# Weight splits and rotary tables made once in the global stage and fetched at layer borders, with the last global norm placed beside the first units

## What is computed

```python
h = _layernorm(x) * (1 + ca) + sa
x = x + ga * attention(h, Wq, bq, Wk, bk, Wv, bv)   # one head, all 1024 tokens
h = _layernorm(x) * (1 + cb) + sb
x = x + gb * ffn(h)
# ffn: six layers, each
y = attn_layer(shift_tokens(y), Wqkv[i], ...) + y   # 16 heads of 64, windows of 32 with the one before
y = ffn_layer(shift_tokens(y), W1[i], W2[i], ...) + y
```

## Time and profile before

| | us |
|---|---|
| median of 3 executions (3318.55 to 3324.52) | 3323.32 |
| the profiled execution | 3324.42 |
| its span, first to last instruction | 3322.6 |
| TensorE busy (matmuls) | 3216.3, 97% |
| VectorE busy | 2647.6, 80% |
| ScalarE busy | 2454.8, 74% |
| GpSimd busy | 2301.0, 69% |
| HBM read / written | 20.48 MB / 2.10 MB |

### The profile page before, as it was taken

The page is one execution under the profiler, slowest core; times in us unless marked ns, Lnnn a source line. Parts: engine busy times, 40 slices in busy tenths (PEclk is TensorE's granted clock), DMA queues, the critical chain, the costliest instruction groups (busy, mean ns, idle before and its releaser), DMA issues. The chain is left out here.

```text
span 3322.6 us, 149878 instructions
## 1 busy us (share of the span) xinstructions
PE 3216.3 (97%) x62645; PEld 2548.6 (77%) x62645; DVE 2647.6 (80%) x6351; ACT 2454.8 (74%) x5069; POOL 2301.0 (69%) x1518
## 2 busy tenths in 40 slices
PE   7979999999999999999999999999999999999997
PEld 5758878777877777887877787777788777778775
DVE  4658878878888887887877888878888887888884
ACT  3437877777777777777777777778777777777774
POOL 2028777777777776777777777777777777777771
PEclk9989999999999999999999999999999999999998
DMA  2001111211211211211121111121111121111111
GB/s 88 3 3 52 46 41 48 70 40 41 56 46 41 74 42 41 55 45 43 49 66 42 48 49 46 41 71 45 48 47 45 43 68 46 50 41 49 46 41 49
DMA packets 98287, 158.06 MB, mean 48 GB/s; under 512 B 18128, under 2 KB 39632, under 8 KB 96720
## 3 DMA queue, kind: packets, MB, share of 16 engines
q1 hardware_dynamic: 93440, 132.73, 14.7%
q10 hardware_dynamic: 4176, 15.74, 1.4%
HBM read 20.48 MB, written 2.10 MB: 7 GB/s over the span
## 5 line engine op out<-in xcount | busy, mean ns | idle before, releaser
L315 POOL TENSOR_TENSOR qks<-work 128x1024 f32<-128x1024 f32 x384 | 911.2, 2373 | 106.4 <-issue 99.3
L323 POOL TENSOR_TENSOR qkr<-qks,rnorm 128x1024 f32<-128x1024 f32 x384 | 732.0, 1906 | 319.3 <-issue 236.1
L492 ACT ACTIVATE sq<-psum 128x512 f32<-128x512 f32 x768 | 460.3, 599 | 307.9 <-PE psum L734 286.8
L331 POOL TENSOR_TENSOR probn<-prob,psumr 128x512 f32<-128x512 f32 x384 | 401.0, 1044 | 310.0 <-DVE psumr L1104 309.9
L734 PE MATMUL psum<-whi,xhi 128*128 128x512 f32 x1152 | 552.2, 479 | 25.9 <-POOL xlo L340 19.2
L1056 DVE TENSOR_REDUCE ssq<-sq 128x8 f32<-128x512 f32 x768 | 518.8, 676 | 8.1 <-ACT sq L492 7.9
L1080 DVE TENSOR_TENSOR work<-psum,rot 128x512 f32<-128x512 f32 x768 | 508.0, 661 | 9.3 <-POOL qks L315 7.2
L757 PEld LDWEIGHTS psum<-kT,qTs 64*32 64x32 f32 x24576 | 362.9, 107 | 155.5 <-issue 128.0
L1098 DVE TENSOR_REDUCE psumr<-prob 128x8 f32<-128x512 f32 x384 | 261.7, 682 | 268.3 <-ACT prob L544 265.2
L734 PE MATMUL psum<-whi,xlo 128*128 128x512 f32 x1152 | 459.4, 399 | 0.0
L734 PE MATMUL psum<-wlo,xhi 128*128 128x512 f32 x1152 | 456.3, 396 | 0.0
(11 more groups left out here) (129 smaller groups left out, 6111.7 us busy)
## 6 DMA issues: line engine op xcount, KB each, us to landing
vsh<-vtok SPq DMA_DIRECT2D x384, 192.0 KB, 2.4
vsh<-vtok SPq DMA_DIRECT2D x384, 64.0 KB, 2.4
xsh<-xs_in SPq DMA_DIRECT2D x192, 64.0 KB, 2.4
ff_x<-x_mid SPq DMA_DIRECT2D x96, 128.0 KB, 2.4
wqkv<-Wqkv_dram ACTq DMA_DIRECT2D x5, 1536.0 KB, 7.4
wo_next<-Wo_dram ACTq DMA_DIRECT2D x5, 512.0 KB, 10.1
xtok<-x_dram SPq DMA_DIRECT2D x4, 512.0 KB, 11.1
out_dram<-qkr SPq DMA_DIRECT2D x8, 256.0 KB, 2.6
```

The costliest lines, as they stand in the source:

```text
L315: pool.tensor_tensor(qks[:, :, :], rcos, rsin, ALU.add).then_inc(s["add_ready"], 1)
L323: pool.tensor_tensor(qkr[:, n % 2, :, :], qks[:, :, :], rnorm[:, :].unsqueeze(2).to_broadcast([P, 2 * OCT, DH]), ALU.mult).then_inc(s["qkr ...
L331: pool.tensor_tensor(probn[:, :, :], prob[:, n % 2, :, :], psumr[:, n % 2, 1, :].unsqueeze(2).to_broadcast([P, OCT, KEYS]), ALU.mult).then ...
L492: act.activation(sq[:, w * OCT:(w + 1) * OCT, :], bank[w].rearrange("p (h n) -> p h n", n=DH), ACT.Square).then_inc(s[("sqq_ready", "sqk_r ...
```

## The change

All splits and all rotary tables are made by GpSimd in the global stage. Wqkv is laid out on the host in the order of SECTIONS, and fetched in 18 pieces (three a layer) of two sections, through two slots of wraw. GpSimd copies a piece to the high part and subtracts it for the low part (weights_split). The first layer's go to wparts, the later ones' to wstage, from where SP stores them to DRAM (wsplit, 15 stores of 1 MB). Tables of six layers (rotary_gains) go the same way, through rstage to rsplit, the first straight to rot, which is now a whole layer's. Around each border SP fetches six sections, two halves of the table and wo straight into place. wraw, wstage and their like share memory with buffers of the units (kT, vtok, qTs, aoT, qks, prob, probT), so GpSimd waits for the last stores before it clears those (overlays_set).

The statistics and the norm of the next batch come one tile earlier in VectorE's program. The last norm of the last batch goes to its own buffer, xn_last, and its parts stand in the units' loop: VectorE at the end of step 1, TensorE and ScalarE at the end of step 2. xlo of unit 0 comes before its rstd on GpSimd. Value projection of unit 0 waits for it.

```diff
-        rot_raw = sb("rot_raw", [P, TPB, 2, 2, DH])
-        rot = sb("rot", [P, TPI, 2, 2, DH])
-        wqkv = sb("wqkv", [P, 3, INNER])
-        whi = sb("whi", [P, 3, INNER], F32R)
-        wlo = sb("wlo", [P, 3, INNER], F32R)
-        wo_next = sb("wo_next", [P, INNER // P, D])
+        rot = sb("rot", [P, TPB, 2, 2, DH])
+        wparts = sb("wparts", [P, len(SECTIONS), 2, 512], F32R)
+        xn_last = sb("xn_last", [P, TPB, D])
...
@@ SP @@
-            sp.dma_start(wqkv[:, :, :].rearrange("p k n -> p (k n)"), Wqkv[0]).then_inc(s["wqkv_in"], 16)
+            def raw_fetched(j):
+                layer, k = j // PIECES, j % PIECES
+                sp.dma_start(wraw[:, j % 2, :, :].rearrange("p s n -> p (s n)"), Wqkv[layer][:, k * 1024:(k + 1) * 1024]).then_inc(wraw_in[j % 2], 16)
+            def split_stored(j):
+                layer, k = j // PIECES, j % PIECES
+                sp.dma_start(wsplit[layer - 1, 2 * k:2 * k + 2].rearrange("s p n -> p s n"),
+                             wstage[:, j % 2, :, :, :].bitcast(F32).rearrange("p s h n -> p s (h n)")).then_inc(w_stored[j % 2], 16)
+            raw_fetched(0)
+            raw_fetched(1)
...
+            for layer in range(1, DEPTH):
+                sp.wait_ge(s["rot_made"], layer + 1)
+                sp.dma_start(rsplit[layer - 1], rstage[:, layer % 2, :, :].rearrange("p t n -> p (t n)")).then_inc(r_stored[layer % 2], 16)
+            for j in range(DEPTH * PIECES):
+                sp.wait_ge(s["w_lo"], j + 1)
+                if j + 2 < DEPTH * PIECES:
+                    raw_fetched(j + 2)
+                if j >= PIECES:
+                    split_stored(j)
+            def section_renewed(layer, k):
...
+                sp.wait_ge(s[("projq_ready", "projk_ready", "vp_ready")[w]], layer * UNITS - 1 + oc)
+                sp.dma_start(wparts[:, k, :, :].bitcast(F32).rearrange("p h n -> p (h n)"), wsplit[layer - 1, k]).then_inc(wparts_in[k], 16)
+            def rotation_renewed(layer, half):
...
+                sp.wait_ge(s["rotk_ready"], layer * UNITS - (1 - half) * UNROLL)
...
+            def output_renewed(layer):
...
+                sp.wait_ge(s["wo_ready"], layer * TILES)
...
             for step in range(STEPS + 2 * UNROLL):
                 x_half(step)
+                section_renewed(renewed_at(step, 0), SECTION_AT[1, 1])
                 ffn_fetched(block_at(step, 1))
                 values_shifted(step - 4)
+                rotation_renewed(renewed_at(step, -6), 0)
+                section_renewed(renewed_at(step, -2), SECTION_AT[0, 0])
+                section_renewed(renewed_at(step, -2), SECTION_AT[1, 0])
+                section_renewed(renewed_at(step, -1), SECTION_AT[0, 1])
+                section_renewed(renewed_at(step, 1), SECTION_AT[2, 0])
+                section_renewed(renewed_at(step, 2), SECTION_AT[2, 1])
+                rotation_renewed(renewed_at(step, 2), 1)
+                output_renewed(renewed_at(step, 6))
@@ GpSimd @@
+            def rotary_gains(layer):
+                if layer >= 3:
+                    pool.wait_ge(r_stored[layer % 2], 16 * ((layer - 1) // 2))
...
+            def weights_split(j):
+                layer, k, slot = j // PIECES, j % PIECES, j % 2
+                pool.wait_ge(wraw_in[slot], 16 * (j // 2 + 1))
+                if j in (PIECES, PIECES + 1):
+                    pool.wait_ge(r_stored[1], 16 * 3)
+                    pool.wait_ge(r_stored[0], 16 * 2)
+                elif layer:
+                    pool.wait_ge(w_stored[slot], 16 * ((j - PIECES) // 2))
+                parts = wstage[:, slot, :, :, :] if layer else wparts[:, 2 * k:2 * k + 2, :, :]
+                pool.tensor_copy(parts[:, :, 0, :], wraw[:, slot, :, :]).then_inc(s["w_hi"], 1)
+                pool.wait_ge(s["w_hi"], j + 1)
+                pool.tensor_tensor(parts[:, :, 1, :], wraw[:, slot, :, :], parts[:, :, 0, :].bitcast(F32), ALU.subtract).then_inc(s["w_lo"], 1)
             global_inverse(0)
-            for k in range(len(SECTIONS)):
-                weights_low(0, k)
-            for n in range(1, 2 * B):
-                global_inverse(n)
+            pool.wait_ge(s["gain_in"], 16 * 2)
+            pool.wait_ge(s["gvs_ready"], 2)
+            for layer in range(4):
+                rotary_gains(layer)
+            global_inverse(1)
+            pool.wait_ge(s["gxn_ready"], 2)
+            for layer in range(4, DEPTH):
+                rotary_gains(layer)
+            done = 0
+            for n, pieces in ((1, 2), (2, 3), (3, 3), (4, 3), (5, 3), (6, 4)):
+                if n > 1:
+                    global_inverse(n)
+                    pool.wait_ge(s["gxn_ready"], n + 1)
+                for j in range(done, done + pieces):
+                    weights_split(j)
+                done += pieces
+            for half in range(2):
+                pool.wait_ge(w_stored[half], 16 * ((DEPTH * PIECES - PIECES + half) // 2))
+            pool.memset(kT[:, :, 0:WIN], 0.0)
+            pool.memset(vtok[:, 1, :, :], 0.0).then_inc(s["overlays_set"], 1)
+            x_low(0)
+            global_inverse(2 * B - 1)
...
             for step in range(STEPS + 2 * UNROLL):
-                low_renewed(renewed_at(step, -1), 0, 1)
-                low_renewed(renewed_at(step, 0), 2, 3)
-                low_renewed(renewed_at(step, 2), 4)
-                low_renewed(renewed_at(step, 3), 5)
-                rotary_gains(step)
-                x_low(step)
+                if step:
+                    x_low(step)
@@ ScalarE @@
-                weights_fetched(renewed_at(step, -8))
-                output_renewed(renewed_at(step, 6))
-                high_renewed(renewed_at(step, -1), 0, 1)
-                high_renewed(renewed_at(step, 0), 2, 3)
-                high_renewed(renewed_at(step, 2), 4)
-                high_renewed(renewed_at(step, 3), 5)
...
+                if step == 2:
+                    for half in range(2):
+                        normed_second(B - 1, half)
@@ TensorE @@
-                if n % UNITS < UPT:
-                    pe.wait_ge(s["w_lo"], n // UNITS * len(SECTIONS) + ((0, 1), (2, 3), (4, 5))[oc if w < 2 else 2][w if w < 2 else oc] + 1)
+                if n % UNITS < UPT and n >= UNITS:
+                    pe.wait_ge(wparts_in[SECTION_AT[w, oc]], n // UNITS * 16)
...
+                if n == 0 and w == 0:
+                    pe.wait_ge(s["overlays_set"], 1)
...
@@ VectorE @@
-                    if i in (3, 4) and b + 1 < B:
+                    if i in (2, 3) and b + 1 < B:
...
-                    if i == 5 and b + 1 < B:
+                    if i == 4 and b + 1 < B:
                         global_normed(b + 1)
...
             global_stats(B - 1, 0, TPB)
-            global_normed(B - 1)
...
                 rotation(step, 0)
+                if step == 1:
+                    global_normed(B - 1)
```

More of the change, by code:

```diff
@@ L52 @@
 SECTIONS = ((0, 0), (1, 0), (0, 1), (1, 1), (2, 0), (2, 1))
+SECTION_AT = {wo: k for k, wo in enumerate(SECTIONS)}
+PIECES = len(SECTIONS) // 2
 HALF = 2 * P
@@ L185, in build @@
         vsh_in = [sem(f"vsh_in{k}") for k in range(2 * UPT)]
+        wraw_in = [sem(f"wraw_in{k}") for k in range(2)]
+        w_stored = [sem(f"w_stored{k}") for k in range(2)]
+        r_stored = [sem(f"r_stored{k}") for k in range(2)]
+        wparts_in = [sem(f"wparts_in{k}") for k in range(len(SECTIONS))]
+        rot_in = [sem(f"rot_in{k}") for k in range(2)]
         block = ctx.enter_context(nc.Block())
@@ new lines, in _, with x_low @@
+            for half in range(2):
+                pool.wait_ge(w_stored[half], 16 * ((DEPTH * PIECES - PIECES + half) // 2))
+            pool.memset(kT[:, :, 0:WIN], 0.0)
+            pool.memset(vtok[:, 1, :, :], 0.0).then_inc(s["overlays_set"], 1)
+            def x_low(n):
+                if not is_unit(n) or n % 4:
+                    return
+                h = n // 4 % 2
+                part = (slice(None), slice(2 * h, 2 * h + 2), slice(None))
+                pool.wait_ge(s["xhi_ready"], n // 4 + 1)
+                pool.tensor_tensor(xlo[part], xsh[:, h, :].rearrange("p (a n) -> p a n", n=P), xhi[part].bitcast(F32),
+                                   ALU.subtract).then_inc(s["xs_ready"], 1)
@@ L449, in _ @@
                         normed_second(b - 1, i - 2)
-                    if i in (1, 2, 3) and b == 0:
-                        weights_high(0, 2 * i - 2)
-                        weights_high(0, 2 * i - 1)
                     if i == 7 and b + 1 < B:
@@ L455, in _ @@
                             projected(b + 1, n)
-            for half in range(2):
-                normed_second(B - 1, half)
             def attended(n):
@@ L796, in value_projection @@
                 need(pe, "vs_ready", n)
+                if n == 0:
+                    pe.wait_ge(s["gout_ready"], 2 * B)
                 if n % 2:
@@ L902, in _ @@
                 ffn_up(block_at(step, 3))
+                if step == 2:
+                    for half in range(2):
```

(1 more changed line is left out.)

135 lines of the change are left out of this document (57 added, 78 removed).

## The result

| | before | after |
|---|---|---|
| median, us | 3321.44 (4 executions, 3318.55 to 3324.52) | 3278.81 (4 executions, 3277.31 to 3282.98) |
| ratio, 95% interval | | 0.9874 (0.9856 to 0.9891) |
| profiled execution, its span | 3324.42, 3322.6 | 3280.10, 3278.3 |

The forecast was 3282, made from a profiled execution of 3324.42 and a median of 3323.32 over three executions; with a fourth the median of before is 3321.44. The changed kernel is 1.26% faster, and between the profiled spans 44.3 us are gone where the sum said 41.6. The three terms of that sum came out unequally, so the traces are read term by term.

What follows compares the result with a forecast made beforehand. TensorE, busy 97% of the span, was taken as the bound, with gains only where it waits. Borders -36, global stage -2.7 and seam -2.9 sum to -41.6 from 3324.4: 3282.8, for the median 3282, range 3262 to 3306.

Steps and rivals of the forecast that it cites:

- The bound: Whole kernel: TensorE sets a rhythm of 62.51 us per round; work taken from other engines counts only where TensorE waits.
- Borders, -36: Five layer borders: 40 us winnable by removing splits, wo copy and wqkv fetch, less 0.8 each; -25 to -43.
- rival 4: Layer borders: the 43 us are TensorE's own work in another order, so nothing goes there; 3319 us, chance 0.04.
- The 0.6 for the W1/W2 fetch: Layer borders: estimated 0.6 us per border left to ffn_renewed's fetch, which stays on ScalarE's queue.
- The 0.8 for a late x_half: Layer borders: x_half, queued on SP behind q1's fetch, arrives late and costs 0.8 us per border, between 0 and 3.
- Global stage, -2.7: Global stage: earlier statistics and norm gain 3.3 and 1.7 us in batches 0 and 1, lose 2.3 in batch 2; -8 to +8.
- the lock on the values' product: Global stage: VectorE's values' product, both inputs in SBUF, could wait for a GpSimd piece; 2 to 5 us against, with the moved normalisation.
- Seam, -2.9: Between global stage and unit 0: first projection 6.4 us earlier, 3.5 given back in the first units; -9 to +5.
- Fast transfers: Global stage, seam and borders: a fetch and store pair lands in 5.5 us instead of 7.4; 3270 us, chance 0.17.
- Borders keep part of their gap: Layer borders: 4.5 MB per layer of fetches cost 4 us per border instead of 0.8; 3299 us, chance 0.2.
- Nothing at the borders: Layer borders: the gap is TensorE's own work in another order, so nothing is won there; 3319 us, chance 0.04.
- The choking stage: Global stage: slow DRAM stores delay rstd, pieces and last store, 3 us per us; slower than before, 3335 at 25 us, chance 0.04.

Runs made afterwards that it cites:

- e7: The kernel before without later layers' weight splits and wqkv fetches (first layer's Wqkv reused; wo fetch and copy stay): 3289.48 us, ratio 0.9906.
- e8: The kernel before without wo_next, its fetch and its copy (first layer's wo reused; splits stay): 3312.3 us, ratio 0.9974.
- e6: The changed kernel without the W1/W2 fetches of later layers, which use the first layer's: 3278.5 us, ratio 0.9873.
- e10: e4 with section q1's fetch at each border asked for behind x_half instead of ahead of it: 3266.85 us, ratio 0.9838.
- e5: The changed kernel without border fetches of sections, rotary tables and wo (first layer's reused; W1/W2 fetch stays): 3276.68 us, ratio 0.9871.
- e0: The changed kernel measured once more, unaltered, on the chip of e9 and e10: 3280.19 us, ratio 0.9877.
- e1: The changed kernel with the last norm put back in its row between the global stage and unit 0: 3284.9 us, ratio 0.9882.
- e3: The changed kernel with its 18 weight pieces handed out as 2, 3, 4, 2, 4, 3 instead of 2, 3, 3, 3, 3, 4: 3269.62 us, ratio 0.9835.
- e4: e3 plus GpSimd waiting for batch 1's product of the values before its second piece: 3264.34 us, ratio 0.9821.
- e9: The changed kernel with each weight store made twice, to two places, the slot free when both landed: 3290.59 us, ratio 0.9909.

## Why the prediction was right

**The bound.** Right. The rhythm of 62.51 us is unmoved by what GpSimd and ScalarE lost between borders, and the gain is where TensorE waited.

**Borders, -36.** Right in size: over all five borders 45.0 - 6.9 = 38.1 us are gone. e7 shows that the splits hold most, 30.5 us by the medians, and the wo copy has the rest, 7.7 (e8). The prediction read two waits of 4.6 us at a border and counted the whole gap of 8.5 as theirs. It gave no reason for the other 3.9. They were theirs: smaller waits that went with the same work, and the lower clock behind them, some 10 us over five borders. Had they been TensorE's own work, as rival 4 had it, the term would have been far too large, so here it was right without having shown why.

What the term leaves over, 1.4 a border, measured 1.4 in this trace and 0.8 to 1.2 in the others that make the fetches, but its two causes fell. The 0.6 for the W1/W2 fetch is 0 within the spread (e6). The 0.8 for a late x_half was right about ScalarE: at four of the five borders it stood for xsh, 0.2 to 1.25 us, and xhi starts 4.4 to 5.4 us after the issue of x_half, 4.98 in the quiet round of the earlier trace rows. But only 0.2 us of it in all reached TensorE as a wait for xlo, and to move q1's fetch behind x_half gained nothing (e10). What remains is TensorE standing with no recorded releaser, up to 1.1 us at a time, and in the one trace without the border fetches there is none of it (e5). The cause stays open. That the fetches starve TensorE's own fetch of instructions would fit, but no run shows it.

**Global stage, -2.7.** It measured -1.0 in the profiled execution (215.66 to 214.67) and -2.5 in e0. As the stage ends between 213.1 and 216.4 with the change (e1 included) and between 213.3 and 215.7 without, its net effect can't be told from nothing; the parts can be read, above all batch 2, 51.5 to 54.7 us with the change and 48.4 to 49.6 without. The parts, from the last tile of one batch to that of the next, in the profiled executions:

| | predicted | measured |
|---|---|---|
| to the end of batch 0 | -3.3 | -4.9 (75.39 to 70.52) |
| batch 1 | -1.7 | -1.1 (48.37 to 47.29) |
| batch 2 | +2.3 | +5.0 (48.37 to 53.34) |

The mechanism of batch 2 was right to a few tenths: VectorE stood 5.29 us for rstd, predicted 5.6. The term was mis-sized in what follows the stand: it counted TensorE's work behind the normalisation at the pace of before. (It also read eight transposes as 1.7 us where the row has 1.89.) But TensorE stood 4.16 us and then worked at 1.2 GHz for 10 us, before for some 4; e3 takes the stand away, has 2.4 GHz there, and makes batch 2 in 47.33. In batches 1 and 2 the term left out the lock on the values' product. The prediction had named it, priced it at 2 to 5 us and kept it out of the sum. It cost 2.1 us ahead of batch 1 (13.53 to 15.58 from tile to tile) and 0.6 ahead of batch 2 (14.11), in e0 3.7 and 0.3, and e4, which keeps GpSimd away from it, is 5.3 us faster than e3, with a gap of 13.52 instead of 17.29. This is how the exclusion of the SBUF — State Buffer page of the Trainium skill (section Who interferes with whom) looks in a trace: 3.34 us for work of 1.28, begun 0.15 after a subtraction of 2.35. The earlier place of the norm is a gain, as the term said: 3.0 and 3.6 us in the two batches of e4 where little else interferes, 3.3 predicted. VectorE stood 0.56 us for rstd in batch 1, where 1.5 was predicted.

**Seam, -2.9.** The first projection was predicted at 219.2 (221.9 less the stage's 2.7) and started at 218.88, and what it waited for was the last store, as predicted; e9 moves it with the store. So it came 9.4 us earlier than before, of which the stage has 1.0 and the seam 8.4, predicted 6.4. The reason is in the pieces. The last batch's norm came 1.7 us later than predicted (189.91), and the four pieces behind it made that good: the copy takes 1.04 us, near the memset, and not 1.4, so a piece takes 3.4 instead of 3.8, and piece 17 ended at 210.85, predicted 211.0. Its store landed 4.9 us later, predicted 6, and xsh, which should have been in time, took 1.0 of that back. Given back up to the first affine step at 342.79 were 2.5 us (123.91 from the first projection, before 121.37), predicted 3.5; the sums stand 2.4 further apart, and the normalisation in unit 1 took 2.48, predicted 2.1 to 4. The term measured -8.4 + 2.5 = -5.9, and e1, which takes it back, 5.8.

**The sum.** -38.1 - 1.0 - 5.9 = -45.0, and behind the 45 rounds the changed kernel takes 0.7 longer: -44.3, as the spans differ. The stage was forecast 1.7 too well, the seam 3.0 and the borders 2.1 too badly: 3282 against 3278.81. That the three errors partly cancel is luck, and so is the size of the stage's term, which moves by more than its error between executions.

**The rivals.** Fast transfers: the stores landed in 6.4 us, and the stands of 4.85 and 4.92 for them deny it; but in the seam it was nearer, as the last store was there 1.1 us behind the last attention, where the forecast had 4.1 and this rival some 0.3. Borders keep part of their gap: 0.8 to 1.4 each, not 4. Nothing at the borders: e7 and the rounds deny it. The choking stage has its mechanism (e9), but nothing made the stores late enough to turn the sign.

## What to carry to other kernels

Count the rounds of the engine that sets the rhythm, and price a change at what lies beside that rhythm: here two engines are busy 116 us less, and 38 us came of it at the borders. When work is moved to an idle engine, look at what stands behind it in that engine's queue: one number in the schedule of the pieces (e3) and one wait (e4) took 14.5 us more off the median, a third of what the whole change won. Price a stall of TensorE by its length and by the clock behind it: the stand of 4.16 us was followed by 10 us at 1.2 GHz, and a stand of 3.17 us cost the clock in e0 and e3 and not in the changed kernel's first trace.

## What the runs showed of the hardware

- Behind a stand of 4.16 us TensorE's granted clock was 0.51 over 10 us, and 16 matmuls took 3.62 us instead of 2.03. Behind one of 3.16 in the same place before it was 0.50 to 0.84 for some 4 us. With the stand gone and the same DMA traffic (252 against 256 GB/s) the clock was 1.00.
- Waits of 30.9 us in all at and between the borders of before came with a granted clock of 0.83 to 0.93 over 20 us at each border, some 10 us more by estimate. With only the wait for kT taken away (e8) it fell at one border of five in the trace.
- Two VectorE products of 512 elements a lane with both inputs in SBUF took 3.34 us instead of 1.28 beside a GpSimd subtraction; the profile shows this as a longer instruction, not as a wait.
- GpSimd's copy of 1024 elements a lane from f32 to the rounded format takes 1.04 us, its subtraction of the same size 2.35, and its table of 2048 elements 4.52.
- A 1 MB store beside a 512 KB fetch lands 6.4 us after its issue (median of 15), and 8.5 when it is made twice. The 1 MB stores of the tables, which lie otherwise in memory, landed in 3.8 (median of 5), so the size alone doesn't set it. DMA: Bandwidth & Descriptors in the Trainium skill (section Anatomy of one DMA) would give 4.4 for 1 MB by its fit for another kind of queue, an estimate; the measured times decide.
- With the fetches of 512 KB into SBUF left out, 0.5 to 1.1 us a border were gone (one trace against nine), and with them all of TensorE's stands that no semaphore ended. Which resource they share isn't shown.
